# Selective state space tower on one Trainium2 core: a longer ring for the state sums, the skip term on TensorE, and one B product in twelve on GpSimd

## The chip, the core and the metric

The kernel runs on one core of a Trainium2 chip. The metric is the device time of one execution in microseconds (us). Engines are named TensorE (PE in the rows), VectorE (DVE), ScalarE (ACT), GpSimd (POOL) and SyncE (SP, which here only issues DMAs). SBUF is the working memory with 128 partitions, PSUM the memory into which TensorE writes, in eight banks of 512 f32 columns.

## The reference

For 64 images of 196 patches plus one class token (L = 197 tokens, 192 channels):

```
h = patches @ W + b, class token in front
xz = layernorm(h) @ W_in;  x, z = split(xz)            # 384 channels each
x = silu(conv(x, 4 taps) + conv_b)
B, C = split(x @ W_x)                                  # 16 states each
delta = softplus(x @ W_dt + b_dt)
state_t = exp(delta_t * A) * state_(t-1) + (delta_t * x_t) * B_t    # 384 x 16, over 197 steps
y_t = sum over the 16 states of state_t * C_t
y = (y + D * x) * silu(z)
h = h + layernorm(y @ W_out) * gamma + beta
h = h + mixture of 8 experts(layernorm(h))             # switch routing with capacity
```

## The kernel before, in words

The images go in 32 **pairs** (394 columns: two images of 197 tokens). Bodies 0 to 3 are written out, bodies 4 to 29 are thirteen turns of a hardware loop that holds two bodies, 30 and 31 are written out again. Afterwards come the routing and the experts (tiles of 256 tokens), which the change does not touch.

A pair has three blocks of 128 channels (m) and four groups of four states (g), so twelve **units** u = 4 m + g. In a unit the 128 partitions are 4 states times 32 channels, and the columns are 4 channel quarters times 394. A unit goes through the engines like this:

- TensorE, `spread_b` (L967): B of four states is spread over the partitions into the PSUM bank `ps_b`, by a product with the 0/1 matrix `pick`.
- VectorE, `bx` (L1301): (delta x), spread in `rep`, times `ps_b`, into one of the `BUFS` = 4 ring buffers `hb`. This is the **B product**.
- ScalarE, `decays` (L665): exp(A delta) into PSUM, two instructions for each half unit k = 0 to 23. VectorE, `scan` (L1310): the recurrence over one half unit, in place. Decay k waits for scan k - 2.
- GpSimd, `times_c` (L476): the ring buffer times C, in place, 128x1576. This is the **C product**.
- TensorE, `state_sum` (L977): four products with `gather_q` add the four states into `ps_y`, two units behind. VectorE, `take_y` (L1324): after each fourth unit y = ps_y + D x. GpSimd, `gate_y` (L494): times silu(z).

Beside the twelve units of pair i, each engine does in its program order the other work. For pair i + 1: three convolutions (`conv`, L936), the B and C product (`bc`), three delta products (`dt`), three z products (`z`), `softplus_exp`, `softplus_ln`, `softplus_rest`, `make_delta`, C spreads (`spread_c`) and their copies (`copy_c`). For pair i + 2: the token product (`tok`), its statistics, `rstd(.., 1)` on GpSimd, `front_norm` on ScalarE, transposes (`front_t`, `copy_front_t`). For pair i - 1: `out_product`, `out_stats`, `rstd(.., 2)`, `out_norm`, `apply_gamma`, `add_residual`, `row_stats`, `rstd(.., 3)`, `row_norm`, `back_t`, `copy_back_t` and the router's small products. Two PSUM banks (`ps_k2`) serve all these products in turn; the numbers in `K_OF`, `TOKS`, `FT`, `CS` give each its place in that sequence.

All engines run in order and wait on semaphores. TensorE puts into step u the spread of unit u + 1, then the state sum of unit u - 2, then other products; GpSimd in step u puts C product u - 1 and beside it what `body` (L525) lists:

```
if u == 6:
    gate_y(i, r, 0)
if front and u == 7:
    softplus_rest(n)
    make_delta(n, o)
```

delta and delta x go through DRAM to be spread: SyncE stores them (`store_ddu`, 12 DMAs), waits for all, and loads them as `rep` (`load_rep`, L384, 4 DMAs for each m). VectorE's first B product and ScalarE's first decay of each m wait for their loads.

## Time and profile before

| | |
|---|---|
| median of 3 runs (3650.44 to 3656.83) | 3653.36 us |
| the profiled execution | 3660.91 us |
| its span, first to last instruction | 3659.2 us |
| mean granted TensorE clock, share of full speed | 0.815 |
| busy share of TensorE, VectorE, GpSimd, ScalarE | 73%, 70%, 69%, 52% |
| busy share of TensorE's weight loads | 44% |
| the pairs | to about 2800 us of the span |

How to read it: the busy shares are means over the pairs and over the experts. What an engine waits for stands in the timeline and in the chain of waits, which follows the work that ended last back from step to step. Times in the timeline are us from the start of the span. Matmuls in f32 of this kernel show as two passes each. The clock of TensorE has two levels, 1.2 and 2.4 GHz; a granted clock of 1.0 is the high one.

### The profile page before, as it was taken

What the parts mean: (1) busy time and instruction counts of PE and PEld (TensorE: products, weight loads), DVE (VectorE), ACT (ScalarE), POOL (GpSimd) and SP (SyncE); (2) the same over time, 40 slices, a digit from 0 to 9 for tenths busy, and PEclk for the clock granted to TensorE, in tenths of its full rate; (3) what the DMA queues carried; (4) which work ended last, traced back from release to release, by engine and by line L of the source; (5) the groups of instructions that cost most, each with busy time, mean ns of one, the idle gap of its engine ahead of it and who ended that gap; (6) DMA issues with size and microseconds to landing.
All of it is one profiled execution on the core that took longest, in us unless ns stands there. A gap on an engine that the chain in (4) does not pass through costs nothing.

```text
span 3659.2 us, 42816 instructions
## 1 busy us (share of the span) xinstructions
PE 2666.8 (73%) x12304; PEld 1595.0 (44%) x12304; DVE 2559.2 (70%) x2907; ACT 1903.5 (52%) x3720; POOL 2508.8 (69%) x1618
## 2 busy tenths in 40 slices
PE   5677777777777777777777777777775211599998
PEld 3334344444344433333444444444431100488887
DVE  1588888888888888788888888888888474122222
ACT  1566665666666666566665656665664100233343
POOL 0477777777677777777776777777777276476775
PEclk9788788878888888787878888888875555799999
DMA  2344444333333334444444433333333000665664
GB/s 81 80 95 102 105 109 100 88 86 86 86 86 86 86 86 92 93 99 97 100 100 101 94 87 86 86 86 86 86 73 73 14 0 20 136 216 197 204 216 132
DMA packets 165968, 360.21 MB, mean 98 GB/s; under 512 B 43498, under 2 KB 139314, under 8 KB 146145
## 3 DMA queue, kind: packets, MB, share of 16 engines
q1 hardware_dynamic: 145313, 329.76, 37.7%
q0 software_dynamic: 20544, 29.34, 2.6%
q14 instruction: 86, 0.70, 0.1%
q8 instruction: 25, 0.41, 0.0%
HBM read 294.03 MB, written 69.51 MB: 99 GB/s over the span
## 4 chain that ended last, share of the span: by engine, by line
PE 37%; POOL 21%; issue 17%; DVE 13%; ACT 8%; DMA 1%; SPq 1%; POOLq 0%; DVEq 0%; ACTq 0%
PE banks L941 8%; PE banks L1220 6%; POOL arena L480 6%; DVE arena L1316 5%; PE banks L983 5%; DVE arena L1307 4%; PE banks L1204 4%; POOL slot_scratch L612 3%; PE banks L943 3%; ACT banks L676 2%; PE banks L1209 2%; POOL arena L516 2%; POOL arena L523 2%; POOL arena L521 2%; POOL arena L513 2%
## 5 line engine op out<-in xcount | busy, mean ns | idle before, releaser
L480 POOL TENSOR_TENSOR arena<-arena 128x1576 f32<-128x1576 f32 x384 | 1260.1, 3285 | 467.4 <-DVE arena L1316 464.4
L1316 DVE TENSOR_TENSOR_SCAN arena<-banks,arena 128x788 f32<-128x788 f32 x768 | 1364.8, 1792 | 171.2 <-ACT banks L676 136.9
L676 ACT ACTIVATE banks<-arena,neg_a 128x392 f32<-128x392 f32 x1536 | 837.8, 581 | 391.7 <-DVE arena L1316 367.9
L1307 DVE TENSOR_TENSOR arena<-arena,banks 128x1576 f32<-128x1576 f32 x384 | 681.2, 1774 | 90.5 <-issue 60.4
L983 PE MATMUL banks<-arena,gather_q 128*32 128x394 f32 x3072 | 423.9, 631 | 109.3 <-POOL arena L480 109.3
L971 PE MATMUL banks<-arena,pick 128*128 128x394 bf16 x384 | 144.8, 377 | 438.6 <-DVE arena L1307 435.3
L941 PE MATMUL banks<-arena,v_lo 128*128 128x394 f32 x768 | 326.2, 573 | 1.6 <-ACT arena L713 1.6
L683 ACT ACTIVATE arena<-arena 99x192 f32<-99x192 f32 x384 | 181.8, 540 | 254.5 <-POOL arena L474 253.8
L971 PEld LDWEIGHTS banks<-arena,pick 128*128 128x128 bf16 x384 | 40.1, 104 | 610.9 <-DVE arena L1307 596.2
L1562 DVE TENSOR_TENSOR arena<-banks,arena 128x384 f32<-128x384 f32 x57 | 31.8, 559 | 383.4 <-PE banks L1220 383.4
L922 PE MATMUL banks<-wtok,arena 128*99 128x192 f32 x1536 | 269.8, 333 | 10.4 <-DMA arena<-in_x 6.3
L922 PEld LDWEIGHTS banks<-wtok,arena 128*99 128x99 f32 x1536 | 249.1, 169 | 50.8 <-issue 49.9
L958 PE MATMUL banks<-arena,wdt 128*128 128x394 f32 x576 | 242.8, 575 | 0.0
L941 PEld LDWEIGHTS banks<-arena,v_lo 128*128 128x128 f32 x768 | 160.6, 220 | 185.3 <-issue 102.5
L1220 PE MATMUL banks<-arena 128*128 128x192 f32 x1368 | 235.0, 328 | 0.7 <-DVE arena L1562 0.7
L1220 PEld LDWEIGHTS banks<-arena 128*128 128x128 f32 x1368 | 224.1, 191 | 1.4 <-DVE arena L1562 1.0
L872 ACT ACTIVATE arena<-banks 128x256 f32<-128x256 f32 x57 | 22.0, 386 | 364.5 <-PE banks L1191 364.5
L612 POOL DMA_INDIRECT slot_scratch<-arena x128 | 142.9, 1116 | 76.2 <-issue 38.7
L1328 DVE SCALAR_TENSOR_TENSOR arena<-arena,dsk,banks 128x394 f32<-128x394 f32 x96 | 59.4, 619 | 188.7 <-PE banks L983 188.7
L641 POOL DMA_INDIRECT out_tokens<-arena x114 | 116.0, 1018 | 98.2 <-DVE arena L1567 79.0
L469 POOL TENSOR_TENSOR arena<-arena,small 99x4 f32<-99x4 f32 x96 | 19.7, 205 | 231.3 <-DVE arena L1295 231.3
L958 PEld LDWEIGHTS banks<-arena,wdt 128*128 128x128 f32 x576 | 125.2, 223 | 118.0 <-issue 62.6
(195 smaller groups left out, 4601.7 us busy)
## 6 DMA issues: line engine op xcount, KB each, us to landing
arena<-delta_du_scratch SPq DMA_DIRECT2D x384, 394.0 KB, 10.6
arena<-in_w_pack SPq DMA_DIRECT2D x57, 1155.0 KB, 5.4
delta_du_scratch<-arena SPq DMA_DIRECT2D x384, 98.5 KB, 2.2
arena<-in_x SPq DMA_DIRECT2D x32, 1176.0 KB, 13.0
rows_scratch<-arena SPq DMA_DIRECT2D x32, 297.0 KB
rows_scratch<-arena SPq DMA_DIRECT2D x32, 294.0 KB
arena<-in_b SPq DMA_DIRECT2D x57, 96.0 KB, 5.4
arena<-in_conv_w SPq DMA_DIRECT2D x1, 2304.0 KB, 9.0
```

The lines of the kernel that those rows point to most:

```text
L480: pool.tensor_tensor(v[:, :, :], v[:, :, :], c_rep[r][:, u % NG].unsqueeze(1).to_broadcast([P, NQ, N2]), ALU.mult).then_inc(s_mulp, 1)
L612: pool.indirect_dma_start(out=slot_dram, out_offset=bass.IndirectOffsetOnAxis(ap=sidx[r][:, c:c + 1].bitcast(U32), axis=0), in_=sval[r][:, ...
L676: ins = act.activation(o, d, ACT.Exp, scale=neg_a[:, c:c + 1])
L683: ins = act.activation(dst(c), src(c), ACT.Identity, scale=rs[:, c:c + 1], bias=nb[:, c:c + 1])
L922: mm = pe.matmul(v[0:H0, f * DIM:(f + 1) * DIM], patches[:, c, b, f * HSTEP:f * HSTEP + H0], wtok[:, c, :], start=(c == 0), stop=(c == KP ...
L941: pe.matmul(v[:, 0:N2], v_lo[:, k, c], t_lo[:, :, k:k + L], start=(k == 0), stop=False)
L958: mm = pe.matmul(v[:, 0:N2], wdt[:, k, c], xz[r][:, k, :], start=(k == 0), stop=(k == MB - 1))
L971: pe.matmul(ps_b[:, 0:N2], pick[:, u % NG, :], bc3[r], start=True, stop=True).then_inc(s_bb, 1)
L983: mm = pe.matmul(ps_y[q * 32:(q + 1) * 32, 0:N2], gather_q[:, :], hb[u % BUFS][:, q, :], start=(g == 0), stop=(g == NG - 1))
L1220: mm = pe.matmul(ps_out[:, f * DIM:(f + 1) * DIM], hid[g % 2][:, c, f * P:(f + 1) * P], w2[:, c, :], start=(c == 0), stop=(c == KF - 1))
L1307: dve.tensor_tensor(hb[u % BUFS][:, :, :], rep[m][:, 1], ps_b[:, 0:N2].unsqueeze(1).to_broadcast([P, NQ, N2]), ALU.mult).then_inc(s_bx, 1)
L1316: dve.tensor_tensor_scan(v, decay[k % 2], v, 0.0, ALU.mult, ALU.add).then_inc(s_scan, 1)
```

## The change

- `BUFS` goes from 4 to 6 ring buffers, and the state sum of a unit is issued three units behind instead of two (`LAG`). VectorE's `take_y` moves from half units 2, 10, 18 to 5, 13, 21.
- The skip term D x is added by TensorE: a matrix `skip` with D on its diagonal, made once, multiplies x into `ps_y` as the first product of each sum (`state_sum`, g = 0). `take_y` is then ps_y times silu(z), and `gate_y` on GpSimd is gone.
- The B product of unit 9 (`BY_POOL`) is done by GpSimd (`bx_pool`), in step 6, from a copy of spread B that ScalarE makes after unit 1 (`keep_b`; units 1 and 9 share g = 1, so the spread is the same). TensorE leaves out the spread of unit 9.
- GpSimd: `softplus_rest` stands before C product 6, `make_delta` behind it; gamma and residual behind C product 7; `rstd(i + 2, 1)` before C product 8.
- ScalarE: one z copy at half units 14, 17 and 18 each (before: two at 18, one at 20), the whole `out_norm` at 16 (before: halves at 12 and 14), `copy_c` 0 and 1 at 20 (before 22).
- TensorE: the first z product before the first token product, the C spreads 0 and 1 before the front transposes. The PSUM turn numbers follow.

```diff
-BUFS = 4
+BUFS = 6
+LAG = 3
+KEEP = 1
+BY_POOL = 2 * NG + KEEP
+BXS = UNITS - 1
...
+        b_keep = h2_lo.rearrange("p c t -> p (c t)")[:, 0:N2]
...
-        OUT, TOKS, FT, CS, BT, ROUTE = 3, 9, 14, 16, 20, 22
-        K_OF = (0, 1, 2, 5, 6, 7, 8, 11, 12, 13)
+        OUT, BT, ROUTE = 3, 20, 22
+        TOKS, FT, CS = (10, 11), (16, 17), (14, 15, 18, 19)
+        K_OF = (0, 1, 2, 5, 6, 7, 8, 9, 12, 13)
...
+            def bx_pool(n):
+                u = BY_POOL
+                pool.wait_ge(s_rep[u // NG], REP * (n + 1))
+                pool.wait_ge(s_bkeep, n + 1)
+                pool.wait_ge(s_ysum, UNITS * n + u - BUFS + 1)
+                pool.tensor_tensor(hb[u % BUFS][:, :, :], rep[u // NG][:, 1], b_keep.unsqueeze(1).to_broadcast([P, NQ, N2]),
+                                   ALU.mult).then_inc(s_bxp, 1)
...
-            def gate_y(n, r, m):
-                pool.wait_ge(s_yev, MB * n + m + 1)
-                if m == 0:
-                    pool.wait_ge(s_z, n + 1)
-                pool.tensor_tensor(y[:, m, :], y[:, m, :], xz[r][:, MB + m, :], ALU.mult).then_inc(s_ysz, 1)
...
-                    if back and u == 2:
-                        gate_y(i - 1, o, 2)
                     if back and u == 5:
                         rstd(i - 1, 2)
+                    if front and u == 7:
+                        softplus_rest(n)
+                    if tokens and u == 9:
+                        rstd(i + 2, 1)
                     if u:
                         times_c(i, r, u - 1)
...
-                    if u == 6:
-                        gate_y(i, r, 0)
+                    if u == BY_POOL - 3:
+                        bx_pool(i)
                     if front and u == 7:
-                        softplus_rest(n)
                         make_delta(n, o)
-                    if tokens and u == 8:
-                        rstd(i + 2, 1)
-                    if back and u == 7:
+                    if back and u == 8:
                         apply_gamma(i - 1)
                         add_residual(i - 1, o)
...
+            def keep_b(n):
+                act.wait_ge(s_bx, bx_count(n, KEEP) + 1)
+                need(act, s_lgmm, n - 1)
+                act.activation(b_keep, ps_b[:, 0:N2], ACT.Copy).then_inc(s_bkeep, 1)
...
+                if u == KEEP + 1:
+                    pe.wait_ge(s_bkeep, n + 1)
...
                 if g == 0:
                     need(pe, s_yev, MB * n + m)
+                    pe.wait_ge(s_x, n + 1)
+                    pe.matmul(ps_y[:, 0:N2], skip[:, m, :], xz[r][:, m, :], start=True, stop=False,
+                              skip_group_check=True).then_inc(s_dx, 1)
...
+                        if u + 1 != BY_POOL:
+                            spread_b(i, r, u + 1)
...
-                    if u >= 2:
-                        state_sum(i, u - 2)
+                    if u >= LAG:
+                        state_sum(i, r, u - LAG)
...
-                dve.scalar_tensor_tensor(out=y[:, m, :], in0=xz[r][:, m, :], scalar=dsk[:, m:m + 1],
-                                         in1=ps_y[:, 0:N2], op0=ALU.mult, op1=ALU.add).then_inc(s_yev, 1)
+                dve.tensor_tensor(y[:, m, :], xz[r][:, MB + m, :], ps_y[:, 0:N2], ALU.mult).then_inc(s_yev, 1)
...
-                        if k == 2:
+                        if k == 5:
                             take_y(i - 1, o, 2)
...
-                    if k in (10, 18):
-                        take_y(i, r, (k - 10) // 8)
+                    if k in (13, 21):
+                        take_y(i, r, (k - 13) // 8)
```

The order of instructions, in the middle of a pair, on GpSimd. Before, from C product 4 to C product 7 (128x1576: C product, 128x394: the rest of B and C at L486, the gate at L498, 128x1182: softplus at L513 and L516, 128x3x394: delta at L521 and L523, 99 rows: gamma and residual):

```order
L480 TENSOR_TENSOR arena<-arena 128x1576
L486 TENSOR_TENSOR arena<-arena 128x394
L480 TENSOR_TENSOR arena<-arena 128x1576
L498 TENSOR_TENSOR arena<-arena 128x394
L480 TENSOR_TENSOR arena<-arena 128x1576
L513 TENSOR_TENSOR arena<-arena 128x1182
L516 TENSOR_TENSOR arena<-arena 128x1182
L521 TENSOR_TENSOR arena<-arena 128x3x394
L523 TENSOR_TENSOR arena<-arena 128x3x394
L502 TENSOR_TENSOR arena<-arena,gam 99x768
L508 TENSOR_TENSOR arena<-arena 99x4x192
L480 TENSOR_TENSOR arena<-arena 128x1576
```

In the changed kernel, the same stretch (L493 is the C product, L501 the B product of unit 9, L528 and L531 softplus, L536 and L538 delta):

```order
L493 TENSOR_TENSOR arena<-arena 128x1576
L507 TENSOR_TENSOR arena<-arena 128x394
L493 TENSOR_TENSOR arena<-arena 128x1576
L501 TENSOR_TENSOR arena<-arena 128x1576
L528 TENSOR_TENSOR arena<-arena 128x1182
L531 TENSOR_TENSOR arena<-arena 128x1182
L493 TENSOR_TENSOR arena<-arena 128x1576
L536 TENSOR_TENSOR arena<-arena 128x3x394
L538 TENSOR_TENSOR arena<-arena 128x3x394
L493 TENSOR_TENSOR arena<-arena 128x1576
L517 TENSOR_TENSOR arena<-arena,gam 99x768
L523 TENSOR_TENSOR arena<-arena 99x4x192
```

The gate has gone and a B product stands in its place; C product 6 has moved between softplus and delta, and C product 7 before gamma and residual.

TensorE at the end of a pair, before (L971 is the B spread, L983 the state sum, L975 the C spreads, L1003 and L1004 the row transposes):

```order
L975 MATMUL banks<-arena,pick 128x394 x2
L971 MATMUL banks<-arena,pick 128x394
L983 MATMUL banks<-arena,gather_q 32x394 x4
L975 MATMUL banks<-arena,pick 128x394 x2
L1003 MATMUL banks<-ident,arena 128x99
L1004 MATMUL banks<-ident,arena 64x99
```

And in the changed kernel (L990 B spread, L1001 the skip product, L1005 state sum, L994 C spreads, L1025 and L1026 row transposes; ahead of it stand the front transposes, L949 and L950):

```order
L949 MATMUL banks<-ident,arena 128x99
L950 MATMUL banks<-ident,arena 64x99
L990 MATMUL banks<-arena,pick 128x394
L1001 MATMUL banks<-arena,skip 128x394
L1005 MATMUL banks<-arena,gather_q 32x394 x4
L994 MATMUL banks<-arena,pick 128x394 x2
L1025 MATMUL banks<-ident,arena 128x99
L1026 MATMUL banks<-ident,arena 64x99
```

The first two C spreads have moved ahead of the front transposes, and the skip product stands between the B spread and the state sum.

## Rows read from the trace of the kernel before

**Rows 1.** The page: busy times of the engines, and a DMA issue.

```profile
PE 2666.8 (73%) x12304; PEld 1595.0 (44%) x12304; DVE 2559.2 (70%) x2907; ACT 1903.5 (52%) x3720; POOL 2508.8 (69%) x1618
...
arena<-delta_du_scratch SPq DMA_DIRECT2D x384, 394.0 KB, 10.6
```

**Rows 2.** Timeline of SyncE's queue: start, duration, line, what is moved, count.

```profile
1483.47 0.64 SPq L366 DMA_DIRECT2D arena<-in_x  x1
...
1556.56 3.57 SPq L388 DMA_DIRECT2D arena<-delta_du_scratch  x8
...
1570.90 0.64 SPq L366 DMA_DIRECT2D arena<-in_x  x1
...
1655.54 0.64 SPq L366 DMA_DIRECT2D arena<-in_x  x1
```

**Rows 3.** Busy us in a turn: PE, PEld, DVE, ACT, POOL; then clock, DMA share, GB/s.

```profile
1483.47:1655.54 172.07, 132.34 (x578) 71.11 (x577) 142.81 (x137) 106.30 (x199) 125.67 (x70) 0.83 0.41 91
```

**Rows 4.** The chain of waits, 1500 to 1700 us: start, duration, engine and line.

```profile
1521.27 0.20 POOL arena L469
...
1568.56 0.98 ACT arena L683 x2
...
1663.67 0.51 PE banks L971
```

**Rows 5.** Timeline of GpSimd: in brackets idle time before, and its releaser.

```profile
1533.41 3.64 POOL L480 TENSOR_TENSOR arena<-arena 128x1576 f32<-128x1576 f32 x1 [2.12 <-DVE arena L1316]
...
1539.37 2.56 POOL L516 TENSOR_TENSOR arena<-arena 128x1182 f32<-128x1182 f32 x1
...
1550.75 3.23 POOL L480 TENSOR_TENSOR arena<-arena 128x1576 f32<-128x1576 f32 x1
...
1562.48 1.01 POOL L472 TENSOR_TENSOR arena<-arena,small 99x4 f32<-99x4 f32 x1
...
1606.02 0.20 POOL L469 TENSOR_TENSOR arena<-arena,small 99x4 f32<-99x4 f32 x1 [4.87 <-DVE arena L1295]
```

**Rows 6.** Timeline of ScalarE.

```profile
1564.09 0.34 ACT L711 ACTIVATE arena<-banks 128x197 f32<-128x197 f32 x1 [4.12 <-PE banks L933]
...
1567.68 1.85 ACT L683 ACTIVATE arena<-arena 99x192 f32<-99x192 f32 x4
...
1651.94 1.86 ACT L683 ACTIVATE arena<-arena 99x192 f32<-99x192 f32 x4
...
1657.36 2.13 ACT L676 ACTIVATE banks<-arena,neg_a 128x392 f32<-128x392 f32 x4
```

**Rows 7.** Groups of instructions in the turn 1483.47 to 1655.54 us.

```profile
L1316 DVE TENSOR_TENSOR_SCAN arena<-banks,arena 128x788 f32<-128x788 f32 x49 | 87.2, 1793 | 13.0 <-ACT banks L676 10.9
...
L1307 DVE TENSOR_TENSOR arena<-arena,banks 128x1576 f32<-128x1576 f32 x24 | 42.6, 1775 | 4.9 <-issue 4.8
...
L498 POOL TENSOR_TENSOR arena<-arena 128x394 f32<-128x394 f32 x6 | 6.1, 1025 | 6.9 <-DVE arena L1328 6.9
```

**Rows 8.** Timeline of TensorE.

```profile
1529.92 0.87 PE L983 MATMUL banks<-arena,gather_q 128*32 128x394 f32 x8
...
1566.78 0.87 PE L983 MATMUL banks<-arena,gather_q 128*32 128x394 f32 x8
...
1577.35 5.13 PE L941 MATMUL banks<-arena,v_lo 128*128 128x394 f32 x8
...
1584.69 2.91 PE L941 MATMUL banks<-arena,v_lo 128*128 128x394 f32 x8
...
1651.68 1.54 PE L983 MATMUL banks<-arena,gather_q 128*32 128x394 f32 x8
...
1659.84 0.48 PE L1012 MATMUL banks<-sww_hi,arena 128*99 128x8 f32 x2
```

**Rows 9.** Timeline of VectorE.

```profile
1555.65 0.62 DVE L1328 SCALAR_TENSOR_TENSOR arena<-arena,dsk,banks 128x394 f32<-128x394 f32 x1 [3.70 <-PE banks L983]
...
1661.82 1.80 DVE L1307 TENSOR_TENSOR arena<-arena,banks 128x1576 f32<-128x1576 f32 x1 [5.20 <-issue]
```

More of the change, by code:

```diff
@@ L104, in build @@
         gather_q = sb("gather_q", [P, 32])
+        skip = sb("skip", [P, MB, P])
         wdt = sb("wdt", [P, MB, INNER])
@@ L770, in copy_back_t @@
                     need(act, s_lgmm, n)
+                    need(act, s_bxp, n + 2 if last is None else last)
                 v = kbank(BT + b, o)
@@ L805, in body @@
                         copy_front_t(i + 2, r, 1)
-                    if front and k == 22:
-                        copy_c(n, o, 0)
-                        copy_c(n, o, 1)
                     if back and k == 22:
@@ L1153, in _ @@
             n = PAIRS - 1
-            state_sum(n, UNITS - 2)
-            state_sum(n, UNITS - 1)
+            for u in range(UNITS - LAG, UNITS):
+                state_sum(n, 1, u)
             pe.wait_ge(s_lg, n)
@@ L1275, in _ @@
                 ins = dve.tensor_copy(gather_q[v, :], ident[v, v])
+            for m in range(MB):
+                ins = dve.tensor_scalar(skip[:, m, :], ident[:, :], dsk[:, m:m + 1], None, ALU.mult)
             ins.then_inc(s_dve0, 1)
@@ L1350, in body @@
                 for k in range(2 * UNITS):
-                    if k % 2 == 0:
+                    if k % 2 == 0 and k != 2 * BY_POOL:
                         bx(i, k // 2)
```

112 lines of the change are left out of this document (60 added, 52 removed).

## The prediction

> **What bounds the kernel now.** Read first the shares of the engines on the page: TensorE 73%, VectorE 70%, GpSimd 69% of the span, so no engine is full and the time lies in how they wait for each other [rows 1]. Second, the cadence of the main part: the load of the next patches marks each pair of images. Two marks in a row are 87.4 us apart and the next 84.6 us, 172.1 us for one turn of the loop [rows 2]. In this turn VectorE is busy 142.8 us, GpSimd 125.7 us, ScalarE 106.3 us, TensorE 132.3 us [rows 3]: per pair of 86.0 us VectorE idles 14.6 us and GpSimd 23.2 us. The 32 pairs hold most of the span; the routing and the experts behind them are not touched.
>
> Third, the chain of waits inside one pair [rows 4]. It is a ring, and I walk it from A, the first small operation of the second norm's deviation on GpSimd (1521.27, then 1606.02, one period of 84.7 us): GpSimd works through C products, softplus, delta, gamma, residual and two more deviations; then ScalarE normalises the rows (1568.56); TensorE transposes them, does the router and the three convolutions (the first from 1577.35, at the low clock [rows 8]); ScalarE does both SiLUs with two table loads; VectorE scans twice and takes the statistics of the output product, which release A again. VectorE's many small waits hang on this ring.
>
> The middle of the ring is GpSimd's burst [rows 5]: from A its third deviation ends at 42.5 us (1562.48 + 1.01 + one small operation: 1563.77). It waited 2.1 us in this stretch, before the C product at 1533.41. But the row norm starts only at 1567.68, A + 46.4, since ScalarE first waited 4.1 us for the front transposes and copied them [rows 6]. In the other pair of the turn it starts at A + 45.9 (1651.94 against 1606.02).
>
> **The change, part by part.**
> 1. *One of twelve products with B moves to GpSimd.* VectorE loses 1.77 us per pair [rows 7]. GpSimd gains one operation of the shape of its C products, 128x1576 with all operands in SBUF: 3.25 us, 3.3 us with the gap to the next [rows 5]. ScalarE gains one copy of 128x394 out of PSUM, at a place where it would wait for the first convolution anyway, so it counts nothing; without that cover it would cost what such a copy takes, under 1 us, in every pair.
> 2. *The skip term on TensorE, the gate on VectorE.* GpSimd loses three gates of 1.02 us per pair [rows 7]. VectorE's y instruction stays one of the same shape (0.62 us), taken at no change. TensorE gains three products 128x394 in f32, each two passes: a quarter of a convolution's group of eight passes, 0.73 us at the high clock (2.91 / 4) and 1.28 us at the low one (5.13 / 4) [rows 8]. Two of the three lie beside scans. The third comes at the last step of a pair, ahead of a state sum, two C spreads and the row transposes.
> 3. *Lag three, ring six.* The state sum whose y was awaited 3.70 us on VectorE [rows 9] comes a unit later, and y later still. These waits vanish in name. Since VectorE is not on the ring there, the gain is nothing by itself: it gets early to where it needs the residual from GpSimd.
> 4. *The new order on GpSimd.* I add up from A. Deviation, C product 4, the rest of B and C, and C product 5 end at A + 9.05 as before. The B product needs state sum 3, which TensorE does after two delta products at A + 9.65 (today's sum at that step runs from 1529.92 to 1530.79, A + 9.5 [rows 8]): the B product ends at 12.9. Softplus starts with the exponential ready at 13.2; its second operation needs VectorE's rounded part, at 17.3 (ScalarE has the decay of scan 13 at A + 9.35, then come scan 13, y, the last part of B and C, B product 7, scan 14 and the rounding: 1.75 + 0.6 + 0.6 + 1.8 + 1.8 + 1.4 [rows 7]). So GpSimd waits 1.8 us. Then: the second softplus operation 2.55, C product 3.3, delta 5.0, C product 3.3, gamma and residual 3.7, deviation 1.7, two C products 6.5, deviation 1.7. The third deviation ends at A + 45.1 against 42.5. The balance says the same: + 3.3 (B product) + 0.6 + 0.3 + 1.8 (new waits) - 1.0 (gate) - 2.1 (old wait) - 0.4 (the one C product of 3.64 us falls back to 3.28) = + 2.5.
> 5. *The new order on ScalarE and TensorE.* The first deviation is now after the residual, at A + 36.9 (before 34.3), and the front norm, decay 20, two C copies, decay 21, front copies and decay 22 follow it: 1.9 + 1.1 + 0.9 + 1.1 + 1.9 + 1.1 end at 44.9. So ScalarE is free just as the deviation is, and the row norm starts at A + 45.15: earlier by 1.3 us in one pair and by 0.8 us in the other. This is what the change buys on the ring, and the gain is small because GpSimd's new product takes back most of what ScalarE's old detour cost.
>
> From the row norm on, the two pairs of a turn differ. In the pair that ends a turn VectorE stands 5.2 us before the first B product of the next, with nothing in the profile that it waits for, and TensorE's next spread at 1663.67, with all convolutions behind it, starts as that product ends [rows 4, 9]. There scan 23 ends at A + 49.85, before at 50.6: **0.75 us** earlier. In the other pair TensorE is the link. Product 11 with B is done at 46.1 (today 45.2, since scan 20 now waits for the front norm); then come B spread, skip, state sum and two C spreads: at the high clock 0.3 + 0.7 + 0.85 + 0.7, so C copy 2 can end at 49.0 and the transposes start at 49.05, before at 49.7: **0.7 us** earlier. At the low clock: 0.45 + 1.3 + 1.5 + 0.85, the transposes start at 50.5, 0.8 us later than today.
>
> Everything behind (router, convolutions, SiLU, to A) is the same work in the same order. The delta store starts 2.3 us later, as delta does; today its eight loads are issued from 1556.56 to 1560.1 [rows 2], land in 10.6 us at the median [rows 1], and the first four are needed at about 1572.3, when the next pair's B product starts; so they have 3 to 5 us of cover. If it were gone, each microsecond more would show in every pair.
>
> **Sum.** 30 whole periods by 0.7 us is 21 us, and behind the last pair the gate of 1.0 us on GpSimd falls away: 22 us. The profiled execution took 3660.9 us at a span of 3659.2 us, so this execution would take 3639 us. The median of the runs shown is 7.5 us below it; 3653.4 - 22 = **3631 us**. A measurement of this kernel tells about 0.2%, 7 us, from no change.
>
> Bounds of the unknown prices: the B product on GpSimd 3.23 us to 3.64 us, the ends of its C products [rows 5]. The additional 0.4 us is covered by the wait for the rounding, so it counts 0 to 0.4 us per pair, 0 to + 12 us. The skip product 0.73 to 1.28 us as said. VectorE's pause at the turn could be 0 to 5.2 us; I take it as it is.
>
> **The rivals.**
> *Low clock at the last step (no change).* For: the same state sum took 0.87 us in one pair (1566.78) and 1.54 us in the other (1651.68) at this place [rows 8], and in my walk TensorE now has nothing to do from about A + 26.5 to 38.5, where today it waits under 4 us. Against: the pair at which it counts is the one with 0.87 us. Then every second pair gains 0.75 us and the others lose 0.8 us: 3653.4 - 1 to - 5, about 3650 us. The Trainium skill, "TensorE: Matmul & The Clock Gate", section "What's actually happening", says that the rate follows from how busy the engine has lately been, and that an idle one is throttled. By that rule the longer pause speaks for this case, 3650 us.
>
> *High clock through the router (larger gain).* The first convolution's eight passes take 5.13 us in one pair and 2.91 us later in the same pair [rows 8]. If the denser work from the second C spreads on lifts the clock earlier, 2.2 us go in every second pair: 15 x 2.2 = 33 us more, 3598 us. For: before the first convolution nothing is changed in the work itself, and the front transposes, skip and state sum now follow each other more closely. Against: the pauses for VectorE and ScalarE between them stay.
>
> *TensorE late in both pairs (slower).* Place: from B product 11 to the first convolution, in both pairs. In the pair at the turn VectorE's 5.2 us hide what TensorE's own turn costs; between its router's end (1659.84 + 0.48) and the spread at 1663.67 lie 3.35 us [rows 4, 8], so its pause may be anything up to that. With the router ended at A + 55.6 (low clock) TensorE decides once its pause is over 1.3 us. At 3.3 us the spread comes at 58.9, today 57.65: + 1.25 us; with + 0.8 us in the other pairs, 15 x 2.05 = 31 us, 3684 us. For: both halves rest on the low clock. Against: ScalarE goes on at 1657.36 without a pause at the turn [rows 6].
>
> *The change does not act as said*: were the B product held back by its two extra waits until the residual is late, GpSimd's chain would be longer at once; its waits are for things done by A + 9.65 at the latest, so this has little.
>
> **How the numbers follow.** Forecast 0.42 (3631 us, itself 3616 to 3645); low clock, no change, 0.20; larger gain 0.19; slower 0.16; not as said 0.03 (near 3653 us or above). The range leaves out the far ends of the outer two: 3590 to 3674 us. Faster by over 0.2%: the forecast, the larger gain and a little of the low clock, 0.64. Within 0.2%: 0.17. Slower: 0.19.
>
> **What would show it.** In the profile after: 11 products with B per pair on VectorE and 13 operations of 128x1576 on GpSimd; VectorE busy about 69.6 us per pair; its waits for y gone, and a wait of 4 to 5 us for the residual before the third statistics; a GpSimd wait of about 1.8 us before the second softplus operation; row norm at A + 45; a turn of about 170.6 us for today's 172.1. Wrong if: the wait for the residual is absent (then GpSimd is not the chain), the row norm starts elsewhere than A + 45, or the transposes start later than A + 50 (then the low clock or TensorE decides).

## The result, and the profile after

| | before | changed |
|---|---|---|
| median (lowest to highest) of 5 runs each | 3653.36 us (3649.91 to 3656.83) | 3672.93 us (3671.07 to 3675.7) |
| span of the profiled execution | 3659.2 us | 3671.6 us |
| 12 turns, from body 4's patch load to body 28's | 2061.5 us | 2074.8 us |

Ratio 1.0058, 95% interval 1.0046 to 1.007: **slower by 0.6%, 20 us**, where 22 us less was forecast. The profiled execution before was 7.5 us above its median, so the spans differ by 12.4 us only.

The page after, the same two places as [rows 1]:

```profile
PE 2594.0 (71%) x12464; PEld 1559.0 (42%) x12464; DVE 2533.8 (69%) x2878; ACT 1912.9 (52%) x3752; POOL 2509.7 (68%) x1554
...
arena<-delta_du_scratch SPq DMA_DIRECT2D x384, 394.0 KB, 11.0
```

VectorE is busy 25 us less. 32 B products fewer and the cheaper y should have given more: 32 x 1.77 + 96 x (0.62 - 0.54) = 64 us. Most of the missing part stands in the groups of VectorE after (whole span):

```profile
L1334 DVE TENSOR_TENSOR arena<-arena,banks 128x1576 f32<-128x1576 f32 x352 | 626.4, 1780 | 119.8 <-issue 84.0 <-DMA arena<-delta_du_scratch 30.1 <-PE banks L990 4.7
L1317 DVE BATCH_NORM_STATS2 arena<-arena 99x6 f32<-99x192 f32 x384 | 107.8, 343 | 166.9 <-POOL arena L523 161.9 <-ACT arena L706 4.9
L1351 DVE TENSOR_TENSOR arena<-arena 32x394 bf16<-32x394 f32 x32 | 55.2, 1724 | 23.6 <-ACT arena L764 22.6
```

and in three groups of the kernel before:

```profile
L1307 DVE TENSOR_TENSOR arena<-arena,banks 128x1576 f32<-128x1576 f32 x384 | 681.2, 1774 | 90.5 <-issue 60.4 <-DMA arena<-delta_du_scratch 29.2
...
L1328 DVE SCALAR_TENSOR_TENSOR arena<-arena,dsk,banks 128x394 f32<-128x394 f32 x96 | 59.4, 619 | 188.7 <-PE banks L983 188.7
...
L1322 DVE TENSOR_TENSOR arena<-arena 32x394 bf16<-32x394 f32 x32 | 18.1, 566 | 23.6 <-ACT arena L748 22.6
```

Two costs have grown. The **last part of B and C** (a subtraction on 32 partitions) takes 1.72 us where it took 0.57: 37 us more in 32 pairs. And the idle time before B products that waited for nothing the profile shows went from 60.4 to 84.0 us: the **pause at the turn** of the loop, now 12 x 7.0 us.

The turn after, to set against [rows 3]; first the pair without the turn, then the one with it, then both:

```profile
1408.31:1493.12 84.81, 64.34 (x297) 34.60 (x293) 71.21 (x68) 53.37 (x100) 62.90 (x33) 0.82 0.42 94
1493.12:1581.89 88.77, 63.00 (x297) 33.72 (x293) 70.26 (x68) 53.46 (x100) 62.87 (x33) 0.81 0.39 88
1408.31:1581.89 173.58, 127.34 (x590) 68.32 (x586) 141.47 (x135) 106.83 (x200) 125.78 (x66) 0.81 0.40 91
```

Timeline of GpSimd after, in the pair with A = 1443.40 (answers to [rows 5]):

```profile
1453.17 3.26 POOL L501 TENSOR_TENSOR arena<-arena 128x1576 f32<-128x1576 f32 x1 [0.73 <-PE banks L1005]
1456.46 2.54 POOL L528 TENSOR_TENSOR arena<-arena 128x1182 f32<-128x1182 f32 x1
1462.01 2.55 POOL L531 TENSOR_TENSOR arena<-arena 128x1182 f32<-128x1182 f32 x1 [3.01 <-DVE arena L1374]
```

and of VectorE, in the same microseconds and at the turn that follows (answers to [rows 9]):

```profile
1454.55 0.54 DVE L1358 TENSOR_TENSOR arena<-arena,banks 128x394 f32<-128x394 f32 x1
1455.12 1.74 DVE L1351 TENSOR_TENSOR arena<-arena 32x394 bf16<-32x394 f32 x1
1456.89 1.80 DVE L1334 TENSOR_TENSOR arena<-arena,banks 128x1576 f32<-128x1576 f32 x1
...
1460.51 1.36 DVE L1374 TENSOR_SCALAR arena<-arena 128x1182 f32<-128x1182 f32 x1
...
1479.72 1.14 DVE L1317 BATCH_NORM_STATS2 arena<-arena 99x6 f32<-99x192 f32 x4 [5.06 <-POOL arena L523]
...
1492.40 1.80 DVE L1345 TENSOR_TENSOR_SCAN arena<-banks,arena 128x788 f32<-128x788 f32 x1 [0.17 <-ACT banks L687]
1501.21 1.80 DVE L1334 TENSOR_TENSOR arena<-arena,banks 128x1576 f32<-128x1576 f32 x1 [7.01 <-issue]
```

The small subtraction begins at 1455.12 while GpSimd's B product runs (1453.17 to 1456.43) and ends 0.43 us after it. Alone it takes 0.57 us, so it stood until GpSimd was nearly or fully done. The last section has the same at two other starting points. The rounding behind it comes at 1460.51 and GpSimd waits 3.0 us for that instead of 1.8. The row norm of ScalarE starts at 1489.52 = A + 46.1, forecast A + 45.15; scan 23 ends at A + 50.8, forecast A + 49.85.

### The profile page after: what moved, and what is told of

Read it like the earlier page. It is cut to its first block, busy times and chain, and to the rows that moved or that the text cites. A ratio compares the mean times of both kernels' runs of the same rounds, so it can differ in the third digit from the quotient of the medians.

```text
span 3671.6 us, 43340 instructions
## 1 busy us (share of the span) xinstructions
PE 2594.0 (71%) x12464; PEld 1559.0 (42%) x12464; DVE 2533.8 (69%) x2878; ACT 1912.9 (52%) x3752; POOL 2509.7 (68%) x1554
## 4 chain that ended last, share of the span: by engine, by line
PE 38%; issue 22%; POOL 15%; DVE 13%; ACT 8%; DMA 1%; SPq 1%; DVEq 0%; POOLq 0%; ACTq 0%
PE banks L958 8%; PE banks L1245 6%; DVE arena L1334 5%; PE banks L1005 4%; PE banks L1229 4%; POOL arena L493 4%; PE banks L975 3%; POOL slot_scratch L623 3%; PE banks L960 3%; DVE arena L1345 3%; ACT banks L687 2%; PE banks L1234 2%; POOL arena L536 2%; POOL arena L523 2%; DVE arena L1351 1%
## 5 line engine op out<-in xcount | busy, mean ns | idle before, releaser
L493 POOL TENSOR_TENSOR arena<-arena 128x1576 f32<-128x1576 f32 x384 | 1248.2, 3254 | 424.9 <-DVE arena L1345 405.7
L1334 DVE TENSOR_TENSOR arena<-arena,banks 128x1576 f32<-128x1576 f32 x352 | 626.4, 1780 | 119.8 <-issue 84.0
L990 PE MATMUL banks<-arena,pick 128*128 128x394 bf16 x352 | 134.7, 383 | 671.9 <-DVE arena L1334 669.3
L1005 PE MATMUL banks<-arena,gather_q 128*32 128x394 f32 x3072 | 411.0, 614 | 2.0 <-POOL arena L493 2.0
L990 PEld LDWEIGHTS banks<-arena,pick 128*128 128x128 bf16 x352 | 37.1, 105 | 760.5 <-DVE arena L1334 717.6
L975 PE MATMUL banks<-arena,wdt 128*128 128x394 f32 x576 | 247.1, 582 | 0.0
L1317 DVE BATCH_NORM_STATS2 arena<-arena 99x6 f32<-99x192 f32 x384 | 107.8, 343 | 166.9 <-POOL arena L523 161.9
L975 PEld LDWEIGHTS banks<-arena,wdt 128*128 128x128 f32 x576 | 127.4, 227 | 121.2 <-issue 67.3
```

The costliest lines, as they stand in the source:

```text
L493: pool.tensor_tensor(v[:, :, :], v[:, :, :], c_rep[r][:, u % NG].unsqueeze(1).to_broadcast([P, NQ, N2]), ALU.mult).then_inc(s_mulp, 1)
L975: mm = pe.matmul(v[:, 0:N2], wdt[:, k, c], xz[r][:, k, :], start=(k == 0), stop=(k == MB - 1))
L990: pe.matmul(ps_b[:, 0:N2], pick[:, u % NG, :], bc3[r], start=True, stop=True).then_inc(s_bb, 1)
L1005: mm = pe.matmul(ps_y[q * 32:(q + 1) * 32, 0:N2], gather_q[:, :], hb[u % BUFS][:, q, :], start=False, stop=(g == NG - 1), skip_group_check ...
L1334: dve.tensor_tensor(hb[u % BUFS][:, :, :], rep[m][:, 1], ps_b[:, 0:N2].unsqueeze(1).to_broadcast([P, NQ, N2]), ALU.mult).then_inc(s_bx, 1)
```

## The experiments

Two theories for the loss: the **collision** (GpSimd's B product holds up a small VectorE operation, and the delay goes round the ring) and the **turn** (the pause is a fetch of the loop's code that stands behind the loads in flight, and the change puts more of these beside it). The rival of the first was that the B product on GpSimd is too much work for it; of the second, that the pause is a fixed price or one covered by other engines.

All ratios are against runs of the kernel before on the same chip. Runs e9 to e12 were made on another chip, where the kernel before took 3745.8 us; they are compared with that alone. (The kernel before took 3655.6 us on the chip of e1 to e4 and 3652.6 us on that of e5 to e8. "Below the changed kernel" is counted from its 3672.9 us, which was not measured again beside these runs, so a few us of such a distance say nothing.) On the chip of e9 to e12 the routing and the experts are slower (1142 us from the last patch load to the end of the span in e10, 1055 us in the trace of before); in its pairs the traces can be laid beside the others, since body 0 of the kernel before took 72.85 us in the trace of before and 72.85 us in run e10 on this one, where the loop doesn't matter yet.

### e1: the last part of B and C one scan earlier

```diff
-                        if k == 13:
+                        if k == 12:
                             last_bc(i + 1, o)
```

> The changed kernel with the last part of B and C on VectorE one half unit earlier (behind scan 12, where it waits for a decay anyway). Port theory: its 1.74 us (0.57 us before the change) came from standing beside GpSimd's B product; it falls to 0.6 us, the rounding and the second softplus operation come 1.7 us earlier, and the row norm starts at A + 45 instead of A + 46.1: 0.5 to 1 us per pair, about 3650 us. Rival: the instruction is slow for another reason, stays at 1.7 us, and the time stays at 3673 us. The pause at the turn of the loop stays at 7.0 us by both.

Measured: **3630.2 us**, ratio 0.9937 (0.992 to 0.9953), 42.7 us below the changed kernel, nearly twice the gain expected. VectorE and GpSimd there, A = 1423.69:

```profile
1432.44 0.72 DVE L1351 TENSOR_TENSOR arena<-arena 32x394 bf16<-32x394 f32 x1
...
1470.84 1.80 DVE L1345 TENSOR_TENSOR_SCAN arena<-banks,arena 128x788 f32<-128x788 f32 x1 [0.16 <-ACT banks L687]
1479.74 1.80 DVE L1334 TENSOR_TENSOR arena<-arena,banks 128x1576 f32<-128x1576 f32 x1 [7.10 <-issue]
```

```profile
1433.35 3.26 POOL L501 TENSOR_TENSOR arena<-arena 128x1576 f32<-128x1576 f32 x1 [0.63 <-PE banks L1005]
...
1440.47 2.55 POOL L531 TENSOR_TENSOR arena<-arena 128x1182 f32<-128x1182 f32 x1 [1.55 <-DVE arena L1374]
```

The subtraction is over before the B product begins, and GpSimd waits 1.55 us instead of 3.01. Its second softplus operation starts at A + 16.8 instead of A + 18.6, the row norm at A + 44.3 instead of A + 46.1 (medians of the pairs). These 1.8 us are more than the collision alone: the edit also takes the subtraction out from between scan 13 and the rounding. Run e2 separates the two. The pause is still 7.1 us.

### e2: all twelve B products on VectorE, no kept copy

```diff
-                    if u == BY_POOL - 3:
-                        bx_pool(i)
...
-                    if k % 2 == 0 and k != 2 * BY_POOL:
+                    if k % 2 == 0:
                         bx(i, k // 2)
```

> The changed kernel with all twelve B products on VectorE; no kept copy. Port theory: as in e1, the last part of B and C falls to 0.6 us, and since GpSimd's B product lay in a stretch in which GpSimd waits for the rounding anyway, the row norm starts at A + 45 here too, about 3650 us. Rival (the B product is what fills GpSimd): the row norm starts 3.3 us earlier, at A + 43 or when ScalarE is free, 3640 us or below. Rival (VectorE needed the relief): slower than 3673 us.

Measured: **3648.2 us**, ratio 0.9981 (0.9972 to 0.9991), the 3650 us expected. The subtraction stands where the change has it and takes 0.57 us again. A = 1429.51:

```profile
1441.20 0.57 DVE L1341 TENSOR_TENSOR arena<-arena 32x394 bf16<-32x394 f32 x1
```

```profile
1446.91 2.55 POOL L531 TENSOR_TENSOR arena<-arena 128x1182 f32<-128x1182 f32 x1 [2.10 <-DVE arena L1364]
```

So the second softplus operation starts at A + 17.4 and the row norm at A + 44.9 (medians): the collision is 1.2 us of the 1.8 us that e1 gave in each pair, the earlier place the other 0.6. At this place the B product on GpSimd costs 25 us (3672.9 against 3648.2). That e1 is 18 us faster than e2 is the worth of the B product on GpSimd and of the earlier place together; no run separates them. The row norm stands here where the forecast had it (A + 45.15), and still the run is only 5 to 7 us below the kernel before, because its pause at the turn is 7.0 to 7.3 us.

### e3: patches and the second group of spread loads behind the turn

```diff
             def body(i, r, front, tok):
+                load_rep(i, r, 1)
+                load_rep(i, r, 2)
                 if tok:
                     load_patches(i + 2)
-                load_rep(i, r, 2)
                 if front:
                     store_ddu(i + 1, 1 - r)
                     load_rep(i + 1, 1 - r, 0)
-                    load_rep(i + 1, 1 - r, 1)
```

> The changed kernel with the load of the next patches and of the second third of the spread delta behind the turn, so that fewer transfers are in flight while VectorE turns. Transfer theory (the pause at the turn is a fetch of code that waits behind the loads): the pause falls from 7.0 us to under 4 us, 13 turns by 3 us, 3635 us. Rival (the pause is a fixed time from VectorE's last half unit): it stays at 7.0 us, and the time at 3673 us.

Measured: **3620.8 us**, ratio 0.9904 (0.9887 to 0.992), 52 us below the changed kernel with the collision still in it. The pause is 2.2 to 3.0 us, once 3.7. VectorE at the same turn:

```profile
1469.93 1.80 DVE L1344 TENSOR_TENSOR_SCAN arena<-banks,arena 128x788 f32<-128x788 f32 x1 [0.17 <-ACT banks L686]
1474.17 1.80 DVE L1333 TENSOR_TENSOR arena<-arena,banks 128x1576 f32<-128x1576 f32 x1 [2.44 <-issue]
```

So most of the pause is the traffic; no instruction of VectorE was touched.

### e4: four bodies in a turn

```diff
-            for i in range(4):
+            for i in range(6):
                 body(i, i % 2, True, True)
-            with dve.Fori(4, PAIRS - 3, 2) as i:
-                body(i, 0, True, True)
-                body(i + 1, 1, True, True)
+            with dve.Fori(6, PAIRS - 5, 4) as i:
+                for j in range(4):
+                    body(i + j, j % 2, True, True)
```

(the same on the other engines)

> The changed kernel with six bodies written out and six turns of four bodies. Turn theory: the pause of 7 us stands once in four pairs; seven pauses less, each of which makes its pair 4.6 us longer than its neighbour: 32 us less, 3641 us. Rival (the long pairs come from something that repeats every second pair, whatever the loop): every second pair stays long, 3673 us.

Measured: **3653.1 us**, ratio 0.9993 (0.9983 to 1.0002), 20 us below the changed kernel. The pause of 6.7 us comes once in four pairs, so it belongs to the turn; a pair that has it lasts 89 to 93 us in place of 88.8, so only 20 of the expected 32 us came back.

### e5: e1 and e3 together

> The changed kernel with both edits of the two best runs: the last part of B and C one scan earlier, and the loads of patches and of the second spread group behind the turn of the loop. Theory 'two separate costs' (GpSimd's B product holds up the last part, 1.74 us against 0.57 us in each pair; and VectorE's pause at the turn lasts as long as the loads are in flight): the gains add, -42.7 and -52 us against the changed kernel's 3672.9, so about 3580 us, with the last part at 0.7 us and the pause at 2 to 3 us. Rival 'both edits repair the same slack' (each only brings VectorE to scan 23 earlier): 3615 to 3625 us, no better than the later loads alone.

Measured: **3564.9 us**, ratio 0.976 (0.9745 to 0.9774): 108 us below the changed kernel and 88 us below the kernel before. The gains add (43 + 52 = 95 us) and somewhat more. Subtraction (0.57 to 0.72 us in every pair but one, where it took 3.38) and pause (2.1 to 2.4 us, twice over 3):

```profile
L1350 DVE TENSOR_TENSOR arena<-arena 32x394 bf16<-32x394 f32 x32 | 25.4, 793 | 23.6 <-ACT arena L763 22.6
```

```profile
1448.76 1.80 DVE L1344 TENSOR_TENSOR_SCAN arena<-banks,arena 128x788 f32<-128x788 f32 x1 [0.16 <-ACT banks L686]
1452.75 1.80 DVE L1333 TENSOR_TENSOR arena<-arena,banks 128x1576 f32<-128x1576 f32 x1 [2.19 <-issue]
```

### e6: the kernel before with e3's edit

> The kernel before with its patches and second spread group loaded behind the turn. There scan 23 waits 1.8 us for ScalarE ahead of the pause. Theory 'the pause is a fetch behind the loads that begins when the engine comes to the end of the turn, so ScalarE's lateness lies beside part of it': the pause of 5.2 us falls to about 0.5 to 1.5 us, 12 turns by 4 us = -48 us plus something in the four written-out bodies, about 3605 us. Rival 'the pause in the kernel before was covered by TensorE or ScalarE, and only the changed kernel exposed it': under 15 us gained, 3640 us or more.

Measured: **3627.6 us**, ratio 0.9936 (0.9921 to 0.9952), 25 us below the kernel before: between the two expectations. VectorE:

```profile
1470.39 1.80 DVE L1315 TENSOR_TENSOR_SCAN arena<-banks,arena 128x788 f32<-128x788 f32 x1 [1.84 <-ACT banks L675]
1474.50 1.80 DVE L1306 TENSOR_TENSOR arena<-arena,banks 128x1576 f32<-128x1576 f32 x1 [2.31 <-issue]
```

The pause falls to 2.3 us although scan 23 still waits 1.84 us ahead of it. My idea that this wait had hidden a part of the pause in the kernel before is refuted: then 0.5 us would be left.

Set beside e3 this run also shows what the longer pause costs the change. With the loads behind the turn in both, the changed kernel, collision included, is the faster one by 7 us (3620.8 against 3627.6 us; ratios 0.9904 and 0.9936, on two chips), where with the loads ahead of it it is the slower one by 20.

### e7: the kernel before with e1's edit (control)

> Control: the kernel before with the same edit that brought 42.7 us in the changed one (the last part of B and C on VectorE one scan earlier). Here GpSimd has no B product and the part takes 0.57 us already. Theory 'collision of the two engines': within 0.2% of the kernel before, 3648 to 3660 us. Rival 'the earlier place itself is worth something, in either kernel' (rounding and softplus begin earlier): faster by over 10 us, 3645 us or less.

Measured: **3655.5 us**, ratio 1.0009 (1.0 to 1.0018): nothing, as the theory had it. But the control is weaker than it was meant to be, for the subtraction did not stay at 0.57 us. It now meets another GpSimd operation, the gate, and takes 1.13 us in the mean of the pairs:

```profile
1531.85 1.17 DVE L1322 TENSOR_TENSOR arena<-arena 32x394 bf16<-32x394 f32 x1
```

```profile
1531.56 1.02 POOL L498 TENSOR_TENSOR arena<-arena 128x394 f32<-128x394 f32 x1
```

The rounding still starts 0.5 us earlier (A + 15.8 instead of A + 16.3), and it brings nothing, since GpSimd doesn't wait for the rounding in this kernel. In the changed kernel it does wait, so there the earlier place counts, as e1 against e2 showed. The control doesn't prove that all of e1's gain is the collision.

### e8: the changed kernel without its skip products

```diff
-                    pe.wait_ge(s_x, n + 1)
-                    pe.matmul(ps_y[:, 0:N2], skip[:, m, :], xz[r][:, m, :], start=True, stop=False,
-                              skip_group_check=True).then_inc(s_dx, 1)
```

> The changed kernel without the three skip products (the output lacks the term D x). It measures what the skip term costs on TensorE. By my prediction's step 2 the third one lies at 0.7 us (high clock) to 1.3 to 1.5 us (low clock) on the path in the pair that does not end a turn, and in the other beside VectorE's pause: 15 x 1.5 = 23 us, so about 3650 us. Theory 'TensorE late in both pairs': -1.5 us in every pair, about 3628 us. Theory 'VectorE's and GpSimd's collision alone sets the loss': under 7 us gained, 3666 us or more.

Measured: **3666.0 us**, ratio 1.0044 (1.0029 to 1.006), 7 us below the changed kernel, at the edge of what the third theory allows. The two intervals overlap (1.0029 to 1.006 and 1.0046 to 1.007), so these 7 us are hardly clear of noise. The profiled execution is the fastest one, 3654.5 us; in it the pairs without a turn are 0.85 us shorter (84.53 to 83.68 on the mean of 12), those with one the same (88.37, 88.40), 10 us in 12 turns. The skip term is not the loss.

### e9: the kernel before with its spread loads 4.6 us later

```diff
             def load_rep(n, r, m):
 
                 need(sp, s_scan, 2 * UNITS * (n - 1) + 2 * NG * (m + 1))
+                if r == 0 and m == 0:
+                    need(sp, s_bx, UNITS * (n - 1) + 11)
```

> The kernel before, and in the pair that ends a turn its eight spread loads for the next pair wait in addition for B product 10 of VectorE, about 4.6 us later than today (1468.66 against 1473.3). Nothing else is changed. In the kernel before scan 23 ends 15.9 us after these loads are issued and the pause is 4.8 us; in the changed kernel 12.0 us after them and the pause is 7.0 us. Theory 'the fetch of the loop's first instructions stands behind the loads in flight': with the loads 4.6 us later, 11.3 us ahead of the end of scan 23, the pause becomes 7 us or somewhat more, 12 turns by 2.2 us = +26 us, about 3680 us. Rival 'the pause's length comes with the changed programs of the engines (their code's size or place)': the pause stays at 4.8 to 5.2 us, within 0.2% of before, 3648 to 3662 us.

Measured: **3778.2 us** against 3745.8 us, ratio 1.0094 (1.0071 to 1.0118), 32 us more where 26 were expected. SyncE and VectorE at the turn:

```profile
1487.44 3.72 SPq L390 DMA_DIRECT2D arena<-delta_du_scratch  x8
...
1497.47 0.64 SPq L366 DMA_DIRECT2D arena<-in_x  x1
```

```profile
1496.76 1.80 DVE L1318 TENSOR_TENSOR_SCAN arena<-banks,arena 128x788 f32<-128x788 f32 x1 [1.84 <-ACT banks L678]
1505.87 1.80 DVE L1309 TENSOR_TENSOR arena<-arena,banks 128x1576 f32<-128x1576 f32 x1 [7.31 <-issue]
```

With nothing changed but the moment of eight loads in every second pair, the pause is that of the changed kernel or a little longer (7.0 to 7.6 us). The 12 turns take 2085.3 us, 23.8 us more than in the trace of before.

### e10 and e11: both kernels with the loop written out

```diff
-            for i in range(4):
-                body(i, i % 2, True, True)
-            with dve.Fori(4, PAIRS - 3, 2) as i:
-                body(i, 0, True, True)
-                body(i + 1, 1, True, True)
+            for i in range(30):
+                body(i, i % 2, True, True)
```

> The kernel before with its loop over the pairs written out (all 30 bodies in a row), for comparison with the changed kernel in the same form. Theory 'the pause belongs to the turn of the loop': it is gone, 12 by 5.0 us = -60 us, about 3593 us. Rival 'ScalarE, GpSimd or the transfers set the pair behind it anyway': under 15 us gained.

> The changed kernel with its loop written out. Theory 'the change's loss is the longer pause at the turn (+1.8 us, 12 times) and the rest of the change is worth about nothing as long as the last part is held up': 12 by 7.0 us = -84 us, about 3589 us, level with or a few us below the kernel before in the same form. Rival 'the turn has no part in the loss': still 20 us above the kernel before in the same form.

Measured: before **3706.2 us**, ratio 0.9903 (0.9881 to 0.9926), so 40 us less of the 60 expected; changed **3712.7 us**, 0.9922 (0.9897 to 0.9948), 33 us less than the kernel before with its loop. The changed kernel with its loop was not run on this chip; by its ratio of 1.0058 it would take about 3767 us (an estimate), so some 55 of the 84 us expected came back. The distance between the two kernels is 6.5 us instead of 20. The groups of B products have no pause left, first before, then changed:

```profile
L1295 DVE TENSOR_TENSOR arena<-arena,banks 128x1576 f32<-128x1576 f32 x384 | 680.7, 1773 | 30.3 <-DMA arena<-delta_du_scratch 29.3
```

```profile
L1322 DVE TENSOR_TENSOR arena<-arena,banks 128x1576 f32<-128x1576 f32 x352 | 625.8, 1778 | 36.6 <-DMA arena<-delta_du_scratch 30.9 <-PE banks L981 4.7
...
L1339 DVE TENSOR_TENSOR arena<-arena 32x394 bf16<-32x394 f32 x32 | 54.7, 1709 | 23.6 <-ACT arena L758 22.6
```

The collision stays (1.71 us). Both take 168.3 us for two pairs, so without the turn the collision eats what the rest of the change gives, no more. The 6.5 us lie outside these 24 pairs; 2.7 of them are in body 0 (75.5 against 72.85 us).

### e12: e5 with the loop written out

> The best version so far (last part earlier, loads later: 3564.9 us) with its loop written out. Its pause is still 2.2 us at each of 12 turns: if the turn alone causes it, -26 us, about 3540 us. Rival 'written-out code is fetched behind the same loads, at other places': 3560 us or more.

Measured: **3660.0 us**, ratio 0.9775 (0.9753 to 0.9798), against e5's 0.976 (0.9745 to 0.9774) on its chip. The rival's time came, but not its mechanism: VectorE has no pause of this kind anywhere in the pairs. The 12 turns take 1985.1 us here, 1986.0 us in e5. So a pause of 2.2 us costs nothing that can be measured, presumably because it lies beside other work; which work was not looked for.

### Side by side

Means over the 12 turns from body 4 to 28 of each profiled execution, from patch load to patch load; "with turn" is the stretch that has the pause in it, which comes at its start. Pauses are all 12, the subtraction is the mean of 32.

| | two pairs | with turn | without | pause | subtraction |
|---|---|---|---|---|---|
| before | 171.79 | 86.96 | 84.83 | 4.8 to 5.2 | 0.57 |
| changed | 172.90 | 88.37 | 84.53 | 6.9 to 7.1 | 1.72 |
| e1 subtraction earlier | 170.16 | 86.96 | 83.20 | 7.0 to 7.2 | 0.70 |
| e2 all B on VectorE | 171.29 | 87.65 | 83.64 | 7.0 to 7.3 | 0.57 |
| e9 before, loads delayed | 173.78 | 88.97 | 84.81 | 7.0 to 7.6 | 0.57 |
| e5 both edits | 165.50 | 82.47 | 83.02 | 2.1 to 3.6 | 0.79 |

Why the pause grew in the changed kernel is in the queue of SyncE. Changed:

```profile
1482.20 3.60 SPq L401 DMA_DIRECT2D arena<-delta_du_scratch  x8
...
1493.12 0.64 SPq L379 DMA_DIRECT2D arena<-in_x  x1
1494.23 7.32 SPq L401 DMA_DIRECT2D arena<-delta_du_scratch  x4
```

Before:

```profile
1468.66 3.56 SPq L388 DMA_DIRECT2D arena<-delta_du_scratch  x8
```

Scan 23 ends at 1484.55 before, 15.9 us after these eight loads began to be issued, and at 1494.20 in the changed kernel, 12.0 us after them; in e9 11.1 us after them. The pause is 4.8, 7.0 and 7.3 us. In the changed kernel the loads are issued at A + 38.8 instead of A + 35.2, since delta is made later, and scan 23 ends at A + 50.8 instead of A + 51.1; so more of the loads is still in flight. DMA share and GB/s in the changed kernel's pause, its first 4 us and its last 3:

```profile
1494.20:1498.20 4.00, 2.52 (x24) 2.16 (x24) 0.00 (x1) 3.52 (x10) 3.25 (x1) 0.90 0.95 201
1498.20:1501.21 3.01, 0.00 (x0) 0.00 (x0) 0.00 (x1) 0.00 (x0) 0.00 (x0) 0.50 1.04 345
```

The DMA engines are full throughout (0.95 and 1.04). In those last 3 us all five columns of engines are at zero. The rate rises from 201 to 345 GB/s; in the kernel before it is 345 GB/s over the whole pause (1484.55 to 1489.38). I take 201 GB/s for the spread loads and 345 GB/s for the patches behind them; the profile doesn't name them.

What seems to be the fetch itself can be seen. Among the DMA queues the profile counts one of kind `instruction` (columns: packets, MB, share of the DMA engines). Before, the first 2.6 us of the pause (1484.56 to 1487.20), in which that queue has no packet, and the other 2.2 us, in which it has one:

```profile
q1 hardware_dynamic: 762, 0.86, 97.9%
```

```profile
q1 hardware_dynamic: 949, 0.80, 116.1%
q14 instruction: 1, 0.01, 0.9%
```

And the last 2.3 us of the changed kernel's pause (1498.90 to 1501.21):

```profile
q14 instruction: 1, 0.01, 0.9%
```

At every one of the 12 turns, in before, changed and e9, such a packet of 8 KB starts 2.1 to 2.5 us ahead of VectorE's first B product. What differs is how long VectorE had stood when it started: 2.7 to 3.1 us before, 4.6 to 4.8 us in the changed kernel, 4.5 to 5.3 us in e9, and under 0.4 us in e3, e5 and e6, where the bulk loads come behind the turn. (The profile doesn't say for which engine a packet of this queue is; that it is VectorE's is read from the times.)

The Trainium skill, "Runtime: NRT & Kernel Launch", section "Instruction fetch mechanics", says that a taken branch to code outside the two blocks that an engine holds forces a DMA fetch before it can go on. The traces agree: the pause is there with a loop only (84.0 us in all; none in e11). What the fetch costs behind other transfers the page doesn't say; here it is 2.1 to 3.7 us where the bulk loads begin less than 2 us ahead of it (e3: 1470.52, the pause from 1471.73), and 4.8 to 7.6 us where eight loads of 394 KB were issued 16 to 11 us ahead of it.

## Why the prediction was wrong, point by point

- **Step 1, the B product on GpSimd at 3.3 us.** Right for itself: 3.26 us. What it does to VectorE at that moment was left out.
- **Step 4, the walk on GpSimd: the step that failed.** The prediction let the third deviation follow from "1.75 + 0.6 + 0.6 + 1.8 + 1.8 + 1.4", with 0.6 us for the last part of B and C. Its place was predicted beside the B product (A + 9.65 to 12.9), and it took 1.74 us. The second softplus operation started at A + 18.6 instead of A + 17.3, the wait for the rounding became 3.0 us instead of 1.8, and A to the row norm 46.1 instead of 45.15. The other terms held: in e2, with the subtraction at the planned place and no B product beside it, these two stand at A + 17.4 and A + 44.9. So the mis-sized term is worth 1.2 us in each pair. The B product on GpSimd, with what it holds up, costs 25 us at this place (e2); the 43 us of e1 hold the earlier place of the subtraction as well.
- **"VectorE's pause at the turn could be 0 to 5.2 us; I take it as it is."** The upper bound was wrong. The prediction had delta 2.3 us later and the end of the pair sooner, and weighed this only against the cover of the next pair's first load. It did not ask what else the loads in flight hold up: 12 x 2.0 = 24 us, and 27 us by e3 and e6 (20 us slower against 7 us faster). This is the second step that failed. The loads were issued 3.6 us later after A than before, where 2.3 had been forecast. e1 took 3630 us, next to the forecast of 3631, but that is luck: it has an edit that the change has not (0.6 us in each pair), the longer pause, and gains 1.6 us in each pair without a turn and nothing in one with it, where 0.7 us in both was forecast.
- **Step 5, ScalarE free just as the deviation is.** Right: it waited 0.68 us for it, then normed the rows; the gain there was lost upstream.
- **TensorE at the last step.** The low clock came in the pair without the turn too (state sum 1.54 us at 1580.96, before 0.87), as the rival "low clock at the last step" had it. The transposes started at A + 50.9, forecast 50.5 for the low clock. But from them to the first convolution it took 5.3 us (1583.51 to 1588.82) where it took 6.4 (A + 49.7 to 1577.35): the router's products now ran at 0.32 us a pair of passes up to 1586.27 and at 0.48 us behind it, where the low clock has 0.48 us throughout (1659.84 [rows 8]). So the late start was made up for, and the pair without a turn is even 0.3 us shorter than before (84.53 against 84.83). The third skip product took 1.54 us (1579.48), above step 2's 0.73 to 1.28; all three cost about 7 us in the whole run (e8), hardly clear of noise. (The sum of that rival has a slip: 15 x 0.8 - 15 x 0.75 - 1.0 is about 0, so 3653 us, not 1 to 5 us less.)
- **Rival "TensorE late in both pairs", 3684 us.** Its sign came, and two thirds of its distance (20 of 31 us), but its mechanism did not: TensorE was idle in the last 3 us of the pause, and about 7 us is all that its new products cost.
- **Step 3, waits for y gone.** Right: 188.7 us of them on VectorE became 10.0 us, and 161.9 us now stand before the statistics, for the residual.
- **"Change not acting".** It acted: 352 B products on VectorE, 32 on GpSimd.
- **The written-out bodies.** Forecast as gain in each period. Body 0 is longer by 4.0 us (76.8 against 72.85): there the chain goes straight through rounding, softplus, delta and its stores to the spread loads, with no cover:

```profile
173.55 1.75 DVE arena L1351
...
178.94 1.37 DVE arena L1374
180.45 2.55 POOL arena L531
...
188.67 2.56 POOL arena L538
...
201.83 8.55 DMA arena<-delta_du_scratch
```

(the chain of waits after, 127 to 206 us). In e1 it is 74.9 us and in e2 75.6: a third of the 4.0 us goes with the B product on GpSimd, half with e1's edit.

The account of the 12 turns: 2061.5 us before, - 19.6 us what the change gives with the pause and the place of the subtraction as e1 has them, + 32.9 us the collision and the later place of the subtraction (e1 to changed), 2074.8 us. What the pause took is inside the 19.6: without its + 2 us in each turn the change would have given some 24 us more (an estimate).

What stays open: which of the loads (patches or spread) holds the fetch up, since e3 moved both (e9 delayed the spread loads alone, so these have a part in it, and the patches' part is open); why the low clock reaches the state sum but not the router; and what the B product on GpSimd is worth when nothing meets it and the subtraction keeps its place, since no run has that.

## What to carry to other kernels

Before moving an operation to GpSimd, list what VectorE does in the same microseconds: one small operation with both inputs in SBUF can stand until GpSimd's has ended, and if it sits on the ring the move can cost more than it gives (25 us here); moving it by one scan gave 43 us back. Look at the moved operation in a control run too: in e7 it met another neighbour. A pause that "waits for nothing" at a loop's turn can be a fetch that stands behind your own transfers: look at what the DMA queues carry then, the `instruction` queue too, and try letting bulk loads begin with the turn, not ahead of it (25 us in the kernel before, 52 us in the changed one). And a stall that is "taken as it is" belongs into the sum as soon as the change moves anything that it depends on.

## What the runs showed of the hardware that was not expected

- Two engines in one working memory: a 32x394 subtraction from two SBUF operands takes 0.57 us alone, 0.72 us in e1, 1.17 us in e7, and 1.74 us when it starts 1.95 us into a 3.26 us GpSimd operation. In all three it ends 0.43 to 0.44 us after the GpSimd operation beside it: at 1456.86 after 1456.43 in the changed kernel, at 1533.02 after 1532.58 in e7, and at 1433.16 in e1, where the C product before the B product ends at 1432.72. So it takes what is left of that operation and 0.44 us. The other way round it was in the rows already: of GpSimd's C products the one at 1533.41 took 3.64 us and not 3.25 [rows 5], and the subtraction ran from 1533.37 for 0.57 us. VectorE's B products and scans, which read one operand from PSUM, keep 1.77 and 1.79 us beside GpSimd. The Trainium skill, "SBUF — State Buffer", section "SBUF: two separate sides", has this as an exclusive lock between GpSimd and VectorE instructions with two SBUF inputs, in which the one that starts second stands still. The traces agree in both directions, roughly in size: the C product was lengthened by 0.4 us where it met 0.53 us of the subtraction.
- TensorE's clock is down by the end of the pause: granted 0.90 in its first 4 us, when router products ran, and 0.50 (the low level) in its last 3 us, when TensorE had nothing. In the kernel before it is 0.50 over the whole pause, router products included. In e1 the first convolution behind it took 4.56 us, the next one 2.91.
- Code written out in full has no such pause on VectorE (e10 to e12), and cost no more than the loop once the loads were out of the way (e12).
